# Latents projected from time-major x before the per-example mixing

## The reference, cut to what matters

```python
h = einsum('bct,bcd->bdt', x, weights[condition])      # mixing of channels, per example
q_c = h @ Wq_c.T + bq_c                                # 512 time steps -> 192
kv  = h @ Wkv_c.T + bkv_c                              # 512 time steps -> 64 + 64
# per example and head: softmax(q k^T / sqrt(192)) v, then Wo; x = x + out
# then a convolution over time per channel and a linear layer
```

## Time and profile before

| | |
|---|---|
| median of 3 runs | 772.38 us (770.73 to 773.88) |
| profiled execution, its own time | 769.3 us |
| its span, first to last instruction | 767.5 us |
| PE busy | 751.7 us, 98% |
| DVE busy | 618.5 us, 81% |
| ACT busy | 380.0 us, 50% |
| POOL busy | 200.3 us, 26% |
| granted TensorE clock, mean | 1.000 |

### The profile page before, as it was taken

The page is one execution under the profiler, slowest core; times in us unless marked ns, Lnnn a source line. Parts: engine busy times, 40 slices in busy tenths (PEclk is TensorE's granted clock), DMA queues, the critical chain, the costliest instruction groups (busy, mean ns, idle before and its releaser), DMA issues.

```text
span 767.5 us, 18485 instructions
## 1 busy us (share of the span) xinstructions
PE 751.7 (98%) x7769; PEld 613.4 (80%) x7769; DVE 618.5 (81%) x1109; ACT 380.0 (50%) x675; POOL 200.3 (26%) x203
## 2 busy tenths in 40 slices
PE   9999999999999999999999999999999899999996
PEld 7777686978788787869787786978677699999996
DVE  5676899998998796777769776878889688888887
ACT  2475546546563675655465546545655322222221
POOL 5002020020002010270200000000040788888872
PEclk9999999999999999999999999999999999999999
DMA  9920010010001000000200010002207268888861
GB/s 223 229 76 5 2 59 3 1 59 3 2 2 59 2 1 29 1 4 14 87 1 2 2 56 2 1 2 59 84 2 187 69 142 209 200 208 204 205 132 70
DMA packets 42739, 51.74 MB, mean 67 GB/s; under 512 B 7025, under 2 KB 29601, under 8 KB 42657
## 3 DMA queue, kind: packets, MB, share of 16 engines
q1 hardware_dynamic: 40384, 49.87, 26.0%
q0 software_dynamic: 1056, 0.49, 0.3%
q10 hardware_dynamic: 1216, 0.19, 0.2%
HBM read 41.91 MB, written 8.63 MB: 66 GB/s over the span
## 4 chain that ended last, share of the span: by engine, by line
PE 92%; DVE 6%; ACT 1%; issue 1%; POOL 0%; DVEq 0%
PE ps L730 33%; PE ps L598 9%; PE ps L599 8%; PE ps L600 8%; PE ps L774 6%; PE ps L797 4%; PE ps L1087 4%; PE ps L616 4%; PE ps L1088 4%; PE ps L1056 2%; PE ps L693 1%; PE ps L1044 1%; PE ps L1046 1%; PE ps L1045 1%; PE ps L1070 1%
## 5 line engine op out<-in xcount | busy, mean ns | idle before, releaser
L1188 ACT ACTIVATE qt<-ps,m_bias 128x512 f32<-128x512 f32 x228 | 145.8, 686 | 97.0 <-PE ps L730 97.0
L730 PE MATMUL ps<-q_high,m_high 64*128 64x512 f32 x768 | 165.3, 397 | 0.5 <-issue 0.5
L730 PE MATMUL ps<-q_high,m_low 64*128 64x512 f32 x768 | 161.6, 387 | 0.0
L730 PE MATMUL ps<-q_low,m_high 64*128 64x512 f32 x768 | 113.8, 387 | 0.0
L730 PEld LDWEIGHTS ps<-q_high,m_high 64*128 64x128 f32 x768 | 88.9, 184 | 15.7 <-issue 6.2
L730 PEld LDWEIGHTS ps<-q_high,m_low 64*128 64x128 f32 x768 | 89.1, 184 | 8.9
L1450 DVE TENSOR_TENSOR z_low<-ps,z_high 128x512 fp32r<-128x512 f32 x128 | 79.5, 680 | 13.8 <-ACT z_high L1206 13.8
L730 PEld LDWEIGHTS ps<-q_low,m_high 64*128 64x128 f32 x768 | 81.3, 184 | 9.9
L528 POOL TENSOR_TENSOR o_sum<-o_part,o_part 128x512 f32<-128x512 f32 x7 | 9.1, 1304 | 288.5 <-ACT o_part L1216 288.5
L1193 ACT ACTIVATE sc<-sc 128x512 f32<-128x512 f32 x60 | 38.0, 633 | 76.3 <-DVE sc L1435 76.2
L1206 ACT CAST z_high<-ps 128x512 fp32r<-128x512 f32 x128 | 66.7, 597 | 12.3 <-PE ps L797 8.0
(11 more groups left out here) (294 smaller groups left out, 1652.7 us busy)
## 6 DMA issues: line engine op xcount, KB each, us to landing
x_in<-in_x SPq DMA_DIRECT2D x16, 512.0 KB, 3.7
x_s<-in_x SPq DMA_DIRECT2D x32, 256.0 KB, 5.5
out<-res SPq DMA_DIRECT2D x31, 256.0 KB, 3.3
toep_high<-taps_scratch SPq DMA_DIRECT2D x32, 192.0 KB, 4.2
toep_low<-taps_scratch SPq DMA_DIRECT2D x32, 192.0 KB, 4.8
toep_far<-taps_scratch SPq DMA_DIRECT2D x32, 64.0 KB, 5.5
wq_nope<-in_L_attn_Wq_up SPq DMA_DIRECT2D x2, 768.0 KB, 10.8
wq_nope<-in_L_attn_Wq_up SPq DMA_DIRECT2D x1, 1536.0 KB, 18.1
```

What stands on the lines that cost most here:

```text
L730: mm = pe.matmul(ps[:, fold_bank(u, j) + e, :], weights[rows, (GH * g + j) // 2, c, :], moving[c][rows, :], start=start, stop=stop)
L1188: act.activation(qt[:, j, :], ps[:, fold_bank(u, j) + j % 2, :], ACT.Identity, bias=m_bias[:, h:h + 1]).then_inc(s["qt_done"], 1)
```

## The change

The host gives x in a second layout, `x_groups` (group, time within a tile, tile, token), and the latent weights already turned and joined side by side as `wcT` (time within a tile, tile, 320 features). The kernel splits x itself and the weights into high and low, projects x first with 128 tokens by 128 time steps of it as stationary operand and 320 columns of weights as moving one (`project`, 48 products a group), copies the result `feat` out of PSUM on ACT with the 64 features of c repeated in front, and then mixes it with the block-diagonal `mix` in float32 (`mix_features`, 12 products a group). The transposes of the weights, `first_mixing`, `h_high` and `h_low` are gone. The copy of kv out of PSUM on ACT moves into the next half step, and `below_max(u, 3)` now stands ahead of the copies of q on DVE.

```diff
-            sp.dma_start(wc_raw[:, 0, :], wq_c[0:P, :]).then_inc(s["wc_in"], 16)
...
-            sp.dma_start(x_in[0][:], x_v[:, 0:2, :]).then_inc(s["x_loaded"], 16)
-            sp.dma_start(x_in[1][:], x_v[:, 2:4, :]).then_inc(s["x1_loaded"], 16)
+            for tt in range(TT):
+                sp.dma_start(wcT_raw[:, tt, :], d["wcT"][:, tt, :]).then_inc(wc_in[tt], 16)
+                sp.dma_start(half_tile(x_raw, tt), d["x_groups"][0, :, tt, :]).then_inc(x_loaded[tt], 16)
...
+            def load_x(k):
+                sp.wait_ge(s["feat_ready"], 4 * k)
+                for tt in range(TT):
+                    sp.dma_start(half_tile(x_raw, tt), d["x_groups"][k, :, tt, :]).then_inc(x_loaded[tt], 16)
...
@@ POOL @@
+            def masked(k):
+                if k >= 1:
+                    pool.wait_ge(s["kv_ready"], k)
+                for j in range(2):
+                    pool.wait_ge(gather_in[j], 32 * (k + 1))
+                    pool.tensor_tensor(mix[j][:].rearrange("p g (b e) -> p g b e", b=4),
+                                       gathered[j][:].unsqueeze(2).broadcast_to([P, 2, 4, C]),
+                                       block_of[:].unsqueeze(1).unsqueeze(3).broadcast_to([P, 2, 4, C]),
+                                       ALU.mult).then_inc(s["mix_ready"], 1)
+            pool.wait_ge(s["row_ready"], 1)
+            gather(0)
+            gather(1)
             pool.dma_start(log_in[:, 0:NMODE], d["L0_cond2_log_A_real"]).then_inc(s["ssm_in"], 16)
...
+            masked(0)
             gather(2)
             gather(3)
...
@@ PE @@
+            def projected(k, n, tt, low):
+                left = half_tile(x_low, tt)[:, P * n:P * n + P] if low else x_high[:, tt, P * n:P * n + P]
+                out_n = ps[:, FEAT_BANK[n], 0:FEAT]
+                if low:
+                    return pe.matmul(out_n, left, wcT_high[:, tt, :], start=False, stop=(tt == TT - 1))
+                pe.matmul(out_n, left, wcT_high[:, tt, :], start=(tt == 0), stop=False)
+                return pe.matmul(out_n, left, wcT_low[:, tt, :], start=False, stop=False)
+            def project(k):
+                u = 2 * k - 1
+                for n in range(4):
+                    if n != 2:
+                        pe.wait_ge(s["s_taken"], 4 * u + (1, 2, 0, 4)[n])
+                    else:
+                        pe.wait_ge(s["zl_done"], 8 * (u - 1) + 6)
+                    for tt in range(TT):
+                        if n == 0:
+                            pe.wait_ge(s["xh_done"], 4 * k + tt + 1)
+                        projected(k, n, tt, False)
+                    for tt in range(TT):
+                        if n == 0:
+                            pe.wait_ge(s["xl_done"], 4 * k + tt + 1)
+                        mm = projected(k, n, tt, True)
+                    mm.then_inc(s["feat_ready"], 1)
+            def mix_features(k):
+                pe.wait_ge(s["feat_done"], 4 * k + 4)
+                pe.wait_ge(s["mix_ready"], 2 * k + 2)
+                if k >= 1:
+                    pe.wait_ge(s["s_taken"], 4 * (2 * k - 1) + 3)
+                    pe.wait_ge(s["zl_done"], 8 * (2 * k - 1))
+                for part, made in enumerate(("q_ready", "qca_ready", "kv_ready")):
+                    for n in range(4):
+                        mm = pe.matmul(mixed_in(part)[:, P * n:P * n + P], feat[:, n, P * part:P * part + P],
+                                       mix[n // 2][:, n % 2, :], start=True, stop=True)
+                    mm.then_inc(s[made], 1)
...
@@ PE, odd u @@
-                    mixed_x(i)
-                    mixed_x(i + 1)
                     output(u - 1, 1)
+                    project(i // 2)
                     output(u - 1, 2)
-                    project_ca(i // 2)
-                    project_ab(i // 2)
-                    project_kv(i // 2)
+                    mix_features(i // 2)
                     output(u - 1, 3)
...
@@ ACT @@
+            def x_rounded(k, tt):
+                act.wait_ge(x_loaded[tt], 16 * (k + 1))
+                if k >= 1:
+                    act.wait_ge(s["s_ready"], 4 * (2 * k - 1) + 4)
+                act.copy(x_high[:, tt, :], half_tile(x_raw, tt)).then_inc(s["xh_done"], 1)
+            def feat_taken(k, n):
+                act.wait_ge(s["feat_ready"], 4 * k + n + 1)
+                act.copy(feat[:, n, 64:64 + FEAT], ps[:, FEAT_BANK[n], 0:FEAT])
+                act.copy(feat[:, n, 0:64], ps[:, FEAT_BANK[n], P:QL]).then_inc(s["feat_done"], 1)
...
@@ ACT, even u @@
                     fold(u, 0, 2)
                     if u % 2 == 0:
                         soft(u - 1, 3)
+                        projected_kv(u // 2)
...
@@ ACT, odd u @@
-                    mixed_high(i)
-                    mixed_high(i + 1)
-                    soft(u, 0)
-                    soft(u, 1)
+                    for tt in range(TT):
+                        x_rounded(i // 2, tt)
+                    for n in range(3):
+                        feat_taken(i // 2, n)
+                        soft(u, n)
+                    feat_taken(i // 2, 3)
+                    projected_ab(i // 2)
                     projected_ca(i // 2)
-                    soft(u, 2)
-                    projected_ab(i // 2)
-                    projected_kv(i // 2)
+                    crossed(i // 2)
...
@@ DVE, odd u @@
+                    for tt in range(TT):
+                        x_rest(i // 2, tt)
                     angles(turn[0], turn[1])
-                    mixed_low(i)
-                    mixed_low(i + 1)
                     below_max(u, 0)
                     angles(turn[1], turn[2])
                     below_max(u, 1)
+                    angles(turn[2], turn[3])
+                    below_max(u, 2)
+                    below_max(u, 3)
+                    projected_ab(i // 2)
                     projected_ca(i // 2)
-                    below_max(u, 2)
-                    angles(turn[2], turn[3])
-                    projected_ab(i // 2)
-                    below_max(u, 3)
+                    crossed(i // 2)
```

More of the change, by code:

```diff
@@ L22 @@
 QUADS = NH // 4
+FEAT = QL + KVL + ROPE
 NPAIR = NH // 2
@@ L288, in build @@
     s = {n: mem.sem(n) for n in weight_names + attention_names + taps_names + ffn_names + channel_names}
+    wc_in = [mem.sem(f"wc_in{n}") for n in range(TT)]
+    x_loaded = [mem.sem(f"x_loaded{n}") for n in range(TT)]
     gather_in = [mem.sem(f"gather_in{n}") for n in range(2)]
@@ L322, in build, with half_tile, mixed_in @@
     th_of = lambda hs: theta[:, hs, :].rearrange("p h (x c) -> p h x c", x=4)
[L324 to L330, removed]
+    def half_tile(pair, tt):
+        return pair[tt // 2][:, tt % 2, :]
+    def mixed_in(part):
+        return ps[:, MIXED_BANK[part], :]
     def tiles(tile):
@@ L457, in _ @@
             pool.wait_ge(s["ident_ready"], 2)
[L458 to L461, removed]
             def gather(i):
-                if i >= 4:
+                if i >= 2:
                     pool.wait_ge(s["mix_ready"], i - 1)
@@ L545, in front @@
             def front(u):
-                front_begun(u)
-                front_ended(u)
+                if u % 2 == 0 and u + 2 < NU:
+                    masked(u // 2 + 1)
+                    if u + 4 < NU:
+                        gather(u + 4)
+                        gather(u + 5)
                 if u % 2 == 0 and u >= 2:
@@ L600, in three @@
                 return pe.matmul(out, ll, rh, start=False, stop=stop)
[L602 to L615, removed]
-                            mm = pe.matmul(ps[:, MIX_BANK(i, n), o:o + P], x_in[i % 2][:, g, tt * P:(tt + 1) * P],
-                                           mix_of(i)[:, g, :], start=True, stop=True)
-                    mm.then_inc(s["h_ready"], 1)
@@ L1109, in _ @@
                 if 0 <= c - 3 < C - 1:
[L1110 removed]
+                    through_ffn(c - 3)
             projected_last()
@@ L1241, in _ @@
             act.copy(warm[:], ones[:])
-            for m_ in range(3):
-                act.wait_ge(s["wcT_ready"], m_ + 1)
-                act.copy(wcT_high[:, :, m_, :],
-                         ps[:, BS + m_, :].rearrange("p (t n) -> p t n", t=TT)).then_inc(s["wcT_high_done"], 1)
-            mixed_high(0)
-            mixed_high(1)
+            for tt in range(TT):
+                act.wait_ge(wc_in[tt], 16)
+                act.copy(wcT_high[:, tt, :], wcT_raw[:, tt, :]).then_inc(s["wcT_high_done"], 1)
+                x_rounded(0, tt)
+            for n in range(4):
+                feat_taken(0, n)
+            projected_ab(0)
             projected_ca(0)
-            projected_ab(0)
+            crossed(0)
             lat_taken(0)
```

241 lines of the change are left out of this document (75 added, 166 removed).

## The result

The changed kernel takes 766.94 us (median of 5 runs, 764.55 to 767.71) and the kernel before, on the same chip, 771.12 us (5 runs, 770.73 to 773.88). The ratio is 0.993, 95% interval 0.9905 to 0.9955: 4.2 us, a little more than the 0.5% that I had named as the limit of this measurement. Ten later runs of the same kernel gave 765.78 us, beside 769.89 for the kernel before (ratio 0.9954, interval 0.9938 to 0.997). The profiled execution took 764.55 us, its span 762.7; it is the fastest of its five. The forecast was 769.3 us, the range 760.5 to 775.5.

A forecast was written before the change was run, and what follows sets the result against it. PE was taken to set the pace in the seven odd stretches: four without waits give -6.8 us, u = 1, 3, 5 give +3.7, the start 0, net -3.1 from 772.38 to 769.3 us; range 760.5 to 775.5.

The forecast's parts named there:

- waits eat most of the gain, within 0.5% or a little more: Whole kernel: net -3.1 us after waits, 769.3 us; chance 0.49, own range 766.5 to 772.5.
- PE's work in one stretch: From output(u-1, 0) to fold(u+1), odd u: PE work 9.72 instead of 11.65 us, 1.93 us less.
- The new wait: Before mix_features, PE waits for four features: 3.4, 2.0, 2.75 us at u = 1, 3, 5, none at 7 to 13.
- The step on ACT's order: At u = 1, 3, 5 ACT's fourth feature copy stands behind soft(u, 2), below_max(u, 2) and the angle steps; waits 2.0 to 3.4 us.
- The start: Before fold(0): wq_rope's landing holds products(2), so 0 gain; it can gain only 0.1 or lose 1.1 us.
- The clock rival: Start and u = 1: PE's clock falls in new idle, costing 2.2 to 4.4 us; 771.5 to 773.7 us; chance 0.26.
- The waits appeared: Rival at u = 1, 3, 5: the waits before mix_features don't appear, sum -11.7, time 760.7 us; chance 0.14.
- Mixing matrices: Rival at the start: gathers land late and delay the first mix, +4 to +8 us, 776 to 780; chance 0.08, slower side.
- Weight loads: Rival in project: unhidden loads of 0.19 us bound the short products, 9.1 us, about +5, 777.5 us; chance 0.03.
- Moved work with no price: kv's copy in the next fold, q copies and x DMAs stay covered; without kv's cover 0.3 us each, 2 us in all.

The follow-up runs named there:

- `m_bias` first: The kernel before, with DVE's bias_part(0) moved ahead of the first exponential chain; 770.51 us in one run, against 769.92.
- both edits of the start: Changed kernel with ACT copying features 1 to 3 ahead of soft 1 and 2, bias_part(0) earlier on DVE, and three filling matmuls; 757.44 us, ratio 0.9827.
- again: The changed kernel, unchanged, measured and profiled a second time; 765.78 us (10 runs).
- filled start: The changed kernel with three filling matmuls, one ahead of mix_features(0) and two ahead of turned_weights(0); 768.49 us, ratio 0.9977.
- ACT's order: The changed kernel with ACT's copies of features 1 to 3 ahead of soft(u, 1) and soft(u, 2); 757.72 us, ratio 0.9835.
- angle steps late: The changed kernel with DVE's angle steps of u = 1, 3, 5 behind the four below_max and the copies of q; 763.97 us, ratio 0.9918.

## Why the prediction was right, and where it was not

- **Which case came.** The likeliest case was "waits eat most of the gain, within 0.5% or a little more", 769.3 us. Measured were 766.94 and 765.78: right case, right range, 2.4 us too high at first. Of these 1.3 are the kernel before, which stood at 772.38 for the forecast and at 771.12 beside the change; the change gave -4.2 us, my sum was -3.1.
- **What was luck in it.** The waits and the pace of PE were right by their mechanism. That the sum came so near was in part luck: the clock's falls at u = 1 and 5, which it priced at nothing, cost 1.5 to 1.7 us each, and against them stood waits shorter than forecast, a start that came earlier in both profiles of the changed kernel, and 0.8 us behind `fold(14)` that nothing explains.
- **PE's work in one stretch.** 15.7 us forecast, 15.55 to 15.68 measured at u = 7 to 13. The value between the rows of 256 and 384 columns, 0.148, was measured as 0.147; the mix at 2.62 us as 2.70. By the Trainium skill's smaller fixed cost for a warm matmul ("TensorE: Matmul & The Clock Gate", section "Wait — 56ns, not 53.3ns?") an estimate would be 0.136; the trace disagrees with it at 320 columns too.
- **The new wait.** The step on ACT's order held, with its chain and its places. Forecast 3.4, 2.0, 2.75 and none; measured 2.54, 1.66, 2.38 and none. Each is 0.3 to 0.9 us smaller: at u = 3 `x_rest` ended at 4.6 us as computed (4.65), and the fourth feature was copied at 13.3 instead of 13.5. The stretches of u = 1 and 3 were 19.35 and 17.61 (19.9 and 17.65 forecast). At u = 5 18.4 was forecast and 19.86 came; less the 1.52 us by which the slow mix exceeds 2.70 it would be 18.34.
- **The start: the step that failed.** "So I take 0 for the start; it can gain only 0.1". `fold(0)` came 2.07 us earlier, 2.7 in the second profile. The reason given, that wq_rope lands at 29.1 whatever stands before it, is wrong twice. The landing moves: 28.7 in the kernel before, 26.8 with `m_bias` first, by 27.0 in the changed kernel, by 25.6 in the one with both edits of the start. And it did not come last: the product's own row, one below that of the weight load, names DVE's `m_bias`, which ended 0.3 us behind the landing, and the earlier trace rows lists that wait too. So the earlier end of q, which I had computed (ACT's last copy of q at 21.7 us; measured 21.2, and 21.6 for DVE's last against 24.35 before), was thrown away. As a number the 0 is less wrong than its reason: with the same code the start also lost its gain again, in three profiles of five, and what it is worth on average these runs do not show.
- **The clock rival.** I gave 0.26 to it, at 2.2 to 4.4 us and a time of 771.5 to 773.7. Its mechanism came true, its price was smaller and lay elsewhere. At the odd half steps it fell behind the waits of 2.4 to 2.6 us, in 5 of 6 cases over three profiles (first, again, filled start), never behind the 1.66 us of u = 3, and cost 1.5 to 1.7 us each. In the start it fell in the first profile, behind the wait of 2.33 us ahead of `turned_weights(0)`, and not in the second; between the two `fold(0)` differs by 0.65 us (29.48 against 28.83). The Trainium skill says that a long wait between matmuls sends PE cold ("TensorE: Matmul & The Clock Gate", section "Loop structure matters more than you think"); these traces agree in kind. The time stayed under this rival's, since the falls cost less, the waits were shorter and the start came earlier.
- **The other rivals.** The waits appeared, so 760.7 did not come; once ACT's order removes them it is 757.7. Mixing matrices: POOL had them at 16.8 us, PE waited 1.2 us at 16.96, forecast 17.9. In one profile with the same start they came 2.3 us later (mix at 19.22), so this rival's mechanism exists, far from the 11 us that it needed. Weight loads hide: 0.147 is far below 0.18.
- **Moved work with no price.** Half steps between changed by 0.16 us in all: priced right. From `fold(0)` to the first output of u = 1 it is 0.49 us more, in the second profile 1.24. That had no term in the sum, and its cause is open.

## What to carry to other kernels

When a change turns four small consumers into one that wants all four, look at where the fourth producer stands in its engine's hand-written order, and move it ahead of work that nothing waits for yet: here that was worth 7 to 9 us (ratio 0.993 and 0.9954 without, 0.9835 with it), about twice what removing 13.5 us of PE work gave without it (4.2 us). Then ask the same of the next half step, since a queue that is merely pushed back (the angle steps) comes due later. Before a wait is called a DMA's, read the row of the matmul itself beside that of its weight load, and the time of the landing beside the end of the other engine's work. And a start that a second and third profile of the same code don't repeat is no gain yet.

## What the runs showed that I had not expected

- Behind an idle time of 2.4 to 2.6 us of PE the clock fell, but not in every execution: at u = 1 with 2.54 us it stayed at 1.00, with 2.55 us (again) it fell, same code. Nor did the length of the idle time decide it alone: at the start it fell behind 1.36 us (angle steps late) and 1.72 us (ACT's order), and not behind 1.34 and 2.16 us (again). Of the six profiles with the new start and no filling matmuls the clock fell in the start in five; in the three with them it stayed at 1.00, and no median shows a gain from it.
- In six of the nine profiles with the new start ACT stood still for 1.7 to 6.2 us, ending between 35.6 and 37.9 us, released by nothing that the profile names, with the DMA engines full; in one more it did for 0.24 us, in two not at all. Its cause is open; the kernel before has no such wait.
- A start that differs by 3.0 us at `fold(0)` (28.58 against 31.59) differs by 1.5 us at u = 1, and by 0.45 us in the medians.
